# A recurrent gated-memory cell on one core: a new instruction order, the output gate's tanh apart, an agent input on VectorE and a second product on GpSimd

## What is computed

```python
def step(carry, xy):
    xt, yt = xy
    st, err, gs, mem, h1, c1, h2, c2 = carry
    encoded = jnp.tanh(xt @ We + st @ Ue + be)
    new_state = jnp.tanh(jnp.einsum('bd,cds->bcs', xt, Wx) + jnp.einsum('bs,cst->bct', st, Ws) + bk)
    inp = jnp.concatenate([encoded, err[:, None]], axis=1)
    mem = jnp.concatenate([inp[:, None, :], mem[:, :-1, :]], axis=1)
    a = jax.nn.relu(mem.reshape(b, -1) @ enc_w1 + enc_b1)
    agent_in = jax.nn.relu(a @ enc_w2 + enc_b2)
    h1, c1 = _lstm_cell(agent_in, h1, c1, lstm_wih1, lstm_whh1, lstm_b1)
    h2, c2 = _lstm_cell(h1, h2, c2, lstm_wih2, lstm_whh2, lstm_b2)
    gate = jax.nn.softmax(h2 @ gate_w + gate_b, axis=1)
    theta = _clamp01(jnp.mean(jnp.abs(mem[:, :10, -1]), axis=1) * 2.5)[:, None]
    gate = gate * theta + gs * (1.0 - theta)
    st = jnp.einsum('bc,bcs->bs', gate, new_state)
    pred = _clamp01(st[:, -1])
    err = pred - yt
    return ((st, err, gate, mem, h1, c1, h2, c2), pred)
```

## Time and profile before

| | us |
|---|---|
| median of three runs | 5656.33 |
| span of the profiled execution | 5654.1 |
| GpSimd's product L873, 512 times, mean | 1.277 |
| VectorE's products L769 / L777, 512 times each, mean | 1.220 / 0.679 |
| VectorE's sums L785, 2048 times, mean | 0.681 |
| ScalarE's cell tanh L548, 1024 times, mean | 0.597 |

### The profile page before, as it was taken

The page is one execution under the profiler, slowest core; times in us unless marked ns, Lnnn a source line. Parts: engine busy times, 40 slices in busy tenths (PEclk is TensorE's granted clock), DMA queues, the critical chain, the costliest instruction groups (busy, mean ns, idle before and its releaser), DMA issues.

```text
span 5654.1 us, 184300 instructions
## 1 busy us (share of the span) xinstructions
PE 5444.6 (96%) x67584; PEld 3397.7 (60%) x67584; DVE 4678.1 (83%) x12841; ACT 3830.9 (68%) x9217; POOL 1646.7 (29%) x3589
## 2 busy tenths in 40 slices
PE   7999999999999999999999999999999999999998
PEld 4666666666666666666666666666666666666665
DVE  7888888888888888888888888888888888888887
ACT  5666666666666666666666666666666666666665
POOL 2222222222222222222222222222222222222222
PEclk9999999999999999999999999999999999999999
DMA  2111111111111111111111111111111111111111
GB/s 66 28 29 30 28 31 28 31 28 31 28 31 28 31 28 28 31 28 31 28 31 28 31 28 31 28 29 30 28 31 28 31 28 31 28 31 28 31 28 39
DMA packets 299286, 172.38 MB, mean 30 GB/s; under 512 B 156734, under 2 KB 263882, under 8 KB 298714
## 3 DMA queue, kind: packets, MB, share of 16 engines
q1 hardware_dynamic: 293568, 159.42, 10.8%
q10 hardware_dynamic: 5146, 3.66, 0.2%
HBM read 74.65 MB, written 2.10 MB: 14 GB/s over the span
## 4 chain that ended last, share of the span: by engine, by line
PE 69%; ACT 15%; DVE 12%; issue 4%; DMA 0%; POOL 0%; ACTq 0%; POOLq 0%; DVEq 0%
PE chain L412 17%; PE a_ps L374 10%; PE cand_ps L343 8%; PE cand_ps L334 8%; ACT a_sb L523 6%; PE chain L399 6%; PE a_ps L363 6%; ACT gates L548 5%; DVE cell_in L708 5%; DVE added L694 4%; PE chain L308 4%; PE a_ps L385 4%; PE chain L429 4%; PE cand_ps L329 3%; ACT tanh_c L554 3%
## 5 line engine op out<-in xcount | busy, mean ns | idle before, releaser
L363 PE MATMUL a_ps<-hist,w_hist 125*64 125x512 f16 x12288 | 1700.2, 381 | 24.9 <-DMA w_hist<-enc_table 24.9
L785 DVE TENSOR_REDUCE state<-mixed 128x64 f32<-128x512 f32 x2048 | 1352.6, 681 | 34.1 <-POOL mixed L873 0.7
L541 ACT ACTIVATE cand<-cand_ps 128x512 f32<-128x512 f32 x2048 | 1154.6, 590 | 184.8 <-PE cand_ps L343 184.8
L412 PE MATMUL chain<-cell_in,cell_w 128*64 128x128 f32 x16384 | 1092.8, 276 | 0.7 <-ACT cell_in L531 0.5
L412 PEld LDWEIGHTS chain<-cell_in,cell_w 128*64 128x64 f32 x16384 | 888.3, 136 | 288.2 <-ACT cell_in L531 181.5
L900 POOL TENSOR_TENSOR err_ring<-pred_now,ys 128x8 f32 x512 | 128.6, 251 | 3106.0 <-DVE pred_now L792 3106.0
L548 ACT ACTIVATE gates<-chain 128x512 f32<-128x512 f32 x1024 | 611.4, 597 | 619.8 <-PE chain L412 619.8
L363 PEld LDWEIGHTS a_ps<-hist,w_hist 125*64 125x64 f16 x12288 | 658.6, 110 | 447.2 <-issue 26.0
L554 ACT ACTIVATE tanh_c<-gates 128x128 f32<-128x128 f32 x1024 | 316.7, 309 | 690.0 <-DVE gates L700 690.0
L694 DVE SCALAR_TENSOR_TENSOR added<-gates 128x256 f32<-128x256 f32 x1024 | 435.5, 425 | 419.4 <-ACT gates L548 419.4
L708 DVE SCALAR_TENSOR_TENSOR cell_in<-gates,tanh_c 64x128 f32<-64x128 f32 x2048 | 588.0, 287 | 159.4 <-ACT tanh_c L554 145.6
(11 more groups left out here) (74 smaller groups left out, 6660.7 us busy)
## 6 DMA issues: line engine op xcount, KB each, us to landing
x_sb<-in_x_l SPq DMA_DIRECT2D x260, 256.0 KB, 2.8
hist<-entry_parts SPq DMA_DIRECT2D x2048, 25.0 KB
w_hist<-enc_table SPq DMA_DIRECT2D x258, 128.0 KB, 2.4
y_rows<-in_y_l SPq DMA_DIRECT2D x260, 8.0 KB
ys<-in_y ACTq DMA_DIRECT2D x1, 2048.0 KB, 16.3
preds_out<-preds SPq DMA_DIRECT2D x1, 2048.0 KB, 8.1
cand<-in_encoder ACTq DMA_DIRECT2D x1, 640.0 KB, 3.8
cell_w<-in_cell ACTq DMA_DIRECT2D x2, 256.0 KB, 4.8
```

What stands on the lines that cost most here:

```text
L363: nc.tensor.matmul(a_ps[g][ENC * half:ENC * half + ENC, :], w_hist[0:HROWS, w_slot(u), kk, wp, :], hist[0:HROWS, xp, k, at:at + 512], star ...
L412: last = nc.tensor.matmul(chain[g][rows, P * r:P * r + P], cell_w[c][:, hf, r, :], cell_in[c][:, g, hf, :], start=False, stop=True, skip_g ...
L541: ins = nc.scalar.activation(cand[:, g, q // 2, :, q % 2, :, :].rearrange("p h s c -> p h (s c)"), cand_ps[q][:, :].rearrange("p (h k) -> ...
L785: V.tensor_reduce(state[:, g, hf, 2 * pair:2 * pair + 2, :], mixed[:, pair, hf, :, :, :], AX, ALU.add)\
```

## The change

- `cell_tanhs` takes three gates (384 columns); the output gate has an instruction of its own, `cell_tanh_out` (128 columns), with its own semaphore.
- Of the two halves of the agent input one stays on ScalarE, the other (`agent_input` on VectorE) is a new VectorE instruction that reads PSUM.
- `mix_quarter` on GpSimd is called twice, for quarter 1 and then for quarter 0. `mix` of VectorE is called for quarters 2 and 3 only.
- `history` can be called for single passes and is spread over the TensorE phase in pieces of one to three passes; `state_transpose` stands behind the first pass of the phase, the candidates' bias is a step of its own ahead of cell 0, and TensorE, ScalarE, VectorE and GpSimd have new orders.
- Waits: `q_sum` is counted by half and pair, TensorE waits for the candidates as a group in `candidates_bias`, ScalarE and GpSimd wait for the quarter's own product, `keep_prediction` waits for `prediction`.

The diff, cut to what the steps touch:

```diff
-CAND_ORDER = (2, 1, 3, 0)
-MIX_ORDER = (1, 0)
+CAND_ORDER = (3, 0, 1, 2)
+FIRST_HALF = (0, 0)
+PIECES = ((0, 0), (1, 0), (0, 1))
...
+            def candidates_bias(item):
+                g, n, u = item
+                for q in CAND_ORDER:
+                    pe.wait_ge(q_cand[q], n)
                 for q in range(Q):
                     rows = slice(D_IN * q, D_IN * q + D_IN)
                     nc.tensor.matmul(cand_ps[q][:, :], ones16[rows, :], cand_bias[rows, :],
                                      start=True, stop=False, skip_group_check=True)
+
+            def candidates_x(item):
+                g, n, u = item
...
-            def history(item, kk):
+
+            def history(item, kk, first=0, end=len(PIECES)):
                 g, n, u = item
                 k = HT - 1 - kk
-                for t, (wp, xp) in enumerate(((0, 0), (1, 0), (0, 1))):
+                for t in range(first, end):
+                    wp, xp = PIECES[t]
...
             def encoder1_now(item):
                 g, n, u = item
+                pe.wait_ge(q_err, n)
                 pe.wait_ge(q_enc, n)
-                pe.wait_ge(q_err, n)
...
                 new, cur, old = items
                 if cur:
+                    history(cur, 2, 0, 1)
+                    state_transpose(cur, 0)
+                    state_transpose(cur, 1)
+                    history(cur, 2, 1, 3)
+                    history(cur, 3, 0, 1)
                     encoded_s(cur)
+                if new:
+                    history_waits(new, extra)
+                    history(new, 0, 0, 1)
+                if cur:
+                    history(cur, 3, 1, 2)
                 if old:
                     logit_bias(old)
-                if cur:
-                    history(cur, 3)
+                if new:
+                    history(new, 0, 1, 2)
                 if old:
                     gate_logits(old)
                 if cur:
+                    history(cur, 3, 2, 3)
                     encoder1_now(cur)
-                if new:
-                    history_waits(new, old, extra)
-                    history(new, 0)
+                    bias_of_cell(cur, 0)
+                if new:
+                    history(new, 0, 2, 3)
+                    history(new, 1, 0, 2)
                 if cur:
                     encoder2(cur)
-                    bias_of_cell(cur, 0)
-                if new:
-                    history(new, 1)
+                    candidates_bias(cur)
+                if new:
+                    history(new, 1, 2, 3)
                 if cur:
                     cell_gates(cur, 0)
-                    candidates_x(cur, old, extra)
+                    candidates_x(cur)
                     candidates_s(cur)
+                if new:
+                    encoded_x(new, extra)
+                if cur:
                     bias_of_cell(cur, 1)
-                if new:
-                    encoded_x(new, old, extra)
-                if cur:
                     cell_gates(cur, 1)
-                if new:
-                    state_transpose(new, 0)
-                    state_transpose(new, 1)
-                    history(new, 2)
-
 
...
-            def agent_input(item):
-                g, n, u = item
+            def agent_input(item, hf):
+                g, n, u = item
+                rows = AGENT_ROWS[hf]
                 act.wait_ge(q_inps, n)
-                for hf in range(HF):
-                    rows = AGENT_ROWS[hf]
-                    last = nc.scalar.activation(cell_in[0][rows, g, hf, :], a_ps[g][rows, 0:P], ACT.Relu,
-                                                bias=enc2_bias[rows, 0:1])
-                last.then_inc(q_in, 1)
+                nc.scalar.activation(cell_in[0][rows, g, hf, :], a_ps[g][rows, 0:P], ACT.Relu,
+                                     bias=enc2_bias[rows, 0:1]).then_inc(q_in, 1)
...
                 if q == CAND_ORDER[0]:
                     act.wait_ge(q_candps, n)
-                    act.wait_ge(q_mul[MIX_ORDER[1]], n)
-                    act.wait_ge(q_mulpool, n)
+                if q // 2 == 1:
+                    act.wait_ge(q_mul[1], n)
+                else:
+                    act.wait_ge(q_mulpool[q], n)
...
             def cell_tanhs(item, c):
                 g, n, u = item
                 act.wait_ge(q_cps[c], n)
-                nc.scalar.activation(gates[c][:, g, 0:4, :].rearrange("p r b -> p (r b)"), chain[g][:, :],
+                nc.scalar.activation(gates[c][:, g, 1:4, :].rearrange("p r b -> p (r b)"), chain[g][:, P:4 * P],
                                      ACT.Tanh).then_inc(q_gates[c], 1)
+
+            def cell_tanh_out(item, c):
+                g, n, u = item
+                nc.scalar.activation(gates[c][:, g, 0, :], chain[g][:, 0:P], ACT.Tanh).then_inc(q_out_gate[c], 1)
...
+            def next_hidden(item, hf):
+                g, n, u = item
+                rows = CELL0_OUT[hf]
+                if hf == 0:
+                    act.wait_ge(q_h[0], n)
+                last = nc.scalar.activation(cell_in[0][rows, g, hf, :], cell_in[1][rows, g, hf, :], ACT.Copy)
+                if hf == HF - 1:
+                    last.then_inc(q_hnext, 1)
...
             def phase(items, extra):
                 new, cur, old = items
                 if cur:
-                    agent_input(cur)
-                if old:
-                    next_hidden(old)
-                if cur:
-                    cell_tanhs(cur, 0)
-                    value_tanh(cur, 0)
-                    candidates(cur, 2)
+                    candidates(cur, 0)
                     candidates(cur, 1)
                     cell_tanhs(cur, 1)
                 if new:
                     state_take(new)
                 if cur:
+                    cell_tanh_out(cur, 1)
                     value_tanh(cur, 1)
                 if new:
                     at_least_zero(new)
                     encoded(new)
-                if cur:
-                    candidates(cur, 3)
-                if new:
                     entry_high(new)
                 if cur:
+                    candidates(cur, 2)
                     exponentials(cur)
                 if new:
                     encoder1(new)
                 if cur:
-                    candidates(cur, 0)
+                    next_hidden(cur, 0)
+                if new:
+                    agent_input(new, 0)
+                    cell_tanhs(new, 0)
+                if cur:
+                    next_hidden(cur, 1)
+                if new:
+                    cell_tanh_out(new, 0)
+                    value_tanh(new, 0)
+                    candidates(new, 3)
 
             run_phases(act, phase)
 
...
+            def new_hidden(item, c, hf):
+                g, n, u = item
+                rows = (CELL0_OUT, CELL1_OUT)[c][hf]
+                if hf == FIRST_HALF[c]:
+                    dve.wait_ge(q_tanhc[c], n)
+                    dve.wait_ge(q_out_gate[c], n)
+                last = V.scalar_tensor_tensor(cell_in[1][rows, g, hf, :], gates[c][rows, g, 0, :], 1.0,
+                                              tanh_c[c][rows, g, :], ALU.add, ALU.mult)
+                if hf != FIRST_HALF[c]:
+                    last.then_inc(q_h[c], 1)
+
+            def agent_input(item, hf):
+                g, n, u = item
+                rows = AGENT_ROWS[hf]
+                dve.wait_ge(q_inps, n)
+                V.tensor_scalar(cell_in[0][rows, g, hf, :], a_ps[g][rows, 0:P], enc2_bias[rows, 0:1], 0.0,
+                                ALU.add, ALU.max).then_inc(q_in_high, 1)
...
             def mix(item, pair):
                 g, n, u = item
...
+                dve.wait_ge(q_gate, n)
                 if pair == 1:
-                    dve.wait_ge(q_cand[2], n)
-                    dve.wait_ge(q_cand[3], n)
+                    dve.wait_ge(q_cand[2], n + 1)
+                    dve.wait_ge(q_cand[3], n + 1)
...
-                dve.wait_ge(q_mul[pair], n + GROUPS if pair == MIX_ORDER[1] else n)
-                if pair == 0:
-                    dve.wait_ge(q_mulpool, n + GROUPS)
+                if pair == 1:
+                    dve.wait_ge(q_mul[1], n + GROUPS)
+                else:
+                    for q in range(2):
+                        dve.wait_ge(q_mulpool[q], n + GROUPS)
                 V.tensor_reduce(state[:, g, hf, 2 * pair:2 * pair + 2, :], mixed[:, pair, hf, :, :, :], AX, ALU.add)\
-                    .then_inc(q_sum[hf], 1)
+                    .then_inc(q_sum[hf][pair], 1)
...
             def phase(items, extra):
                 new, cur, old = items
-                if cur:
-                    new_hidden(cur, 0)
                 if old:
+                    fresh_gate(old)
+                    new_gate(old)
+                if cur:
+                    error_sum(cur)
+                    agent_input(cur, 1)
+                if old:
+                    mix(old, 1)
                     mix_sum(old, 0, 1)
```

(75 more changed lines are left out.)

57 lines of the change are left out of this document (21 added, 36 removed).

## The result

The changed kernel takes 5569.15 us (5568.94 to 5569.65, four runs) against 5656.56 for the kernel before in the same session: a ratio of 0.985, 95% interval 0.983 to 0.986. It is faster by 87 us or 0.17 us a phase, where 79 us slower was forecast. The time lies inside the stated range of 5440 to 5860, but on the other side of "no change" and outside the forecast case's own range of 5685 to 5870.

The account below looks back on a forecast made before the run. TensorE's order was taken to bound the 10.945 us phase, with short waits. In the new order VectorE's `cell_terms` waits for GpSimd's second product, giving 11.11: +0.16 x 512 = +82, forecast 5735 us, range 5440 to 5860.

Parts of the forecast that it names:

- the forecast case: VectorE's `added` of cell 0 held for GpSimd's whole second product: period 11.11, 5735 us, own range 5685 to 5870, chance 0.60.
- the candidate ahead of the exponentials: ScalarE: `entry_high` and a candidate tanh precede the exponentials, putting them at 4.77 where the logits would allow 4.44; costs 0.3.
- the two products back to back: GpSimd: quarter 0's product follows quarter 1's after 1.25 us (bounds 1.2 and 1.5), starting at 7.95 and ending at 9.23.
- the product 0.36 + 0.23 later: GpSimd: first product starts 0.36 (`gate_in_sbuf`) plus a 0.23 gap after `gate_in_sbuf` starts, at 6.70.
- the regrouped waits: Waits across engines: they ask for what has long happened, so they were priced at nothing.
- it ends at 9.23 + 0.40: VectorE, cell 0: `cell_terms` stands until the second product ends at 9.23, then ends 0.40 later, at 9.63.
- the collision of `share` with `kept_gate`: VectorE's `share` and `fresh_gate` fall into GpSimd's small instructions: 0 to 0.15 us later, taken as 0.05.
- Rival C: VectorE held, but GpSimd's products come 0.2 earlier: period 10.85 to 10.97, 5605 to 5665 us, chance 0.17.
- Rival B: A long GpSimd product lets VectorE read in between: period 10.52, median 5440, or 5530 with 0.18 more; chance 0.20.
- D: ScalarE late at cell 1 behind three candidate tanhs, 0.48 each; costs nothing unless they slip by 0.4; chance 0.03 with slower.
- The saving of 0.11 at cell 1 by the split tanh: ScalarE: tanh of 384 columns takes 0.49 instead of 0.60, so `cell_terms` of cell 1 starts at 1.61 instead of 1.72.
- ends after 9.06: Condition on GpSimd's second product: if it ends later than 9.06, holding VectorE for it decides, whenever the first cell comes.

Follow-up runs that it names:

- `register_op`: The changed kernel with the sums of quarters 0 and 1 counted by two, so a register instruction again stands between `gate_in_sbuf` and the product: 5646.17 us.

## Why the prediction was wrong

From the second cell at 2999.73, forecast against trace:

| step | forecast | measured |
|---|---|---|
| `encoded_s` | 2.31 | 2.30 |
| logits | 3.43 | 3.51 |
| `encoder1_now` | 4.19 | 3.98 |
| exponentials | 4.77 | 4.74 |
| `fresh_gate` | 5.80 | 5.74 |
| `gate_in_sbuf` | 6.11 | 6.04 |
| next first cell | 6.96 | 6.79 |
| first product | 6.70 | 6.47 |
| `added` of cell 0 starts | 8.62 | 8.45 |
| second product ends | 9.23 | 8.98 |
| `added` ends | 9.63 | 9.26 |
| next second cell | 11.11 | 10.74 |

The prediction failed in the sizes of its sum. The order and the mechanism were read rightly: the candidate ahead of the exponentials, the two products back to back, `added` waiting for the second, and VectorE's relief lost in that wait. The sum was mis-sized by 0.37 us in a case that stood 0.16 above the kernel before, so its sign was wrong. Three terms:

- *"the product 0.36 + 0.23 later"* (0.16 of the 0.37). I took the gap of 0.23 for a cost of the product, and carried it over. It belongs to a register instruction that waits for the gate, and the regrouped waits, which the forecast had at nothing, removed it: 0.07 is left, and with the instruction put back (`register_op`) the gap is 0.24 again and the time 77 us longer. The trace of the kernel before could have told: at the run's end, where the item numbers are constants, the gap is 0.08. GpSimd in the kernel before:

```profile
5638.09 0.32 POOL L861 TENSOR_TENSOR gate<-fresh,kept 128x64 f32<-128x64 f32 x1 [2.58 <-issue]
5638.49 1.26 POOL L873 TENSOR_TENSOR mixed<-cand,gate 128x512 f32<-128x512 f32 x1
```

- *"it ends at 9.23 + 0.40"* (0.12). I added nearly the whole length of `added` (0.42) to the product's end, as if it began only then. Measured are 0.28 and 0.27: the wait covers the first third of it. The earlier trace rows could not have told this. There the later instruction ends 0.27 behind GpSimd's too, but it is only 0.28 to 0.29 long by itself, and it had started 0.06 ahead of GpSimd's end.
- *Upstream* (0.07 up to `gate_in_sbuf`, 0.02 in the second product). 0.03 of it is the exponentials; from them to `fresh_gate` it is 1.00, so the collision of `share` with `kept_gate`, taken at 0.05, costs 0.02 at most.

With both the first and the second term right, the same sum would have given 10.83, or 5600 us: faster. The price of the turn's start, 0.45 us in one phase of ten, was in neither; it makes the mean 10.77 (10.945 less the 0.17 measured) instead of the 10.74 shown.

Rival C came nearest: it had the right mechanism, with "the gap before the first falls" among its conditions. Its lower end of 10.85 or 5605 us stood for products 0.2 earlier; they came 0.23 earlier, and the shorter end of `added` came on top. Rival B fell: without any hold the time is 5377 to 5384, and the trace shows the hold plainly. D cost nothing, as said: the third candidate tanh ends 0.4 us before the cell's tanh is due. The saving of 0.11 at cell 1 by the split tanh is there in the trace, but worth 0.07 a phase; `encoder1_now` came 0.2 earlier than thought, since the logits' block in front of it takes 0.25 rather than 0.54 when a history pass follows at once. This had no part in the result, because the first cell was not what `added` waited for.

The chances put 0.29 on faster. The forecast's border was a second product that "ends after 9.06" (with 0.28 for the rest of `added` instead of 0.40 it would have been 9.18). The forecast had 9.23, the trace has 8.98, and the border and the 9.23 were both a sum of terms known to 0.1 or 0.2.

## What to carry to other kernels

Work handed to GpSimd is not beside VectorE but in its way when a VectorE instruction that reads twice from SBUF starts while it runs. Look at what stands next to the GpSimd instruction, down to its operands, and put one of them in PSUM: this was worth 185 us where the move itself was worth 31, and in the version that computes the whole reference, with a ScalarE instruction more and the call boundary moved, 135. A gap in front of an instruction belongs to the program, not to the instruction: ask which register work or wait stands there before carrying it over, above all once it gets on the path. When a forecast's sign hangs on a difference of 0.16 us between two sums of 11, the terms have to be known better than that, or the chances have to say so.

## What the runs showed of the hardware

`added`, a VectorE instruction with two SBUF operands (128x256, 0.42 us), ends 0.27 to 0.29 us behind a GpSimd product that was running when it started, whether the wait is 0.4 or 1.07 us; with one operand in PSUM it keeps its 0.41 to 0.42. Other sizes were not measured beside a long product. GpSimd's products in the changed kernel keep their 1.26 to 1.29 us, so here the instruction that started later carried the whole cost. And a register instruction of 0.04 us on GpSimd that carries the wait for the gate, with semaphore instructions queued between it and the product, makes the gap ahead of the product 0.23 to 0.24 us instead of 0.07.
